# Depthwise images read out of padded maps in SBUF instead of a DRAM copy

## The reference

```python
x = mamba_fuse(x)                      # layer 0: two Mamba blocks, 1x1 fusion, batch norm, + residual x
g = group_norm(x, 32 groups)           # layer 1
d = [dwconv3(g), dwconv5(g), dwconv7(g)]   # depthwise, one 2-D filter per channel, padding SAME
x = x + conv1x1(concat(d))
t = tokens(x)                          # layers 2 and 3: linear attention, then an MLP in fp8 numbers
```

## Time and profile before

| | before |
|---|---|
| median of three runs | 4153.86 us (4151.6 to 4156.21) |
| the profiled execution | 4153.76 us |
| its span | 4152.0 us |
| PE busy | 3542.9 us |
| DVE busy | 3424.4 us |
| ACT busy | 2398.3 us |
| POOL busy | 2838.0 us |
| preparation | 3058 to 3181 us |
| depthwise loop | 3181 to 3395 us |

### The profile page before, as it was taken

One profiled execution on the slowest core, in us unless ns is written; L12 is line 12 of the kernel. 1 busy time (PEld: TensorE's weight loads), 2 busy tenths in 40 slices (PEclk: granted clock), 3 DMA queues, 4 the chain that ended last, 5 costly groups with the idle time before them and its releaser, 6 DMA issues. The chain is left out here.

```text
span 4152.0 us, 38656 instructions
## 1 busy us (share of the span) xinstructions
PE 3542.9 (85%) x10080; PEld 1452.8 (35%) x10080; DVE 3424.4 (82%) x4323; ACT 2398.3 (58%) x4121; POOL 2838.0 (68%) x2328
## 2 busy tenths in 40 slices
PE   6899999999999999999999999998843878686776
PEld 2333333333333333333333333333311336364563
DVE  3999999999999999999999999999971006767676
ACT  5666766766667766666667766666522222425335
POOL 4988889999998889999988899999840000302113
PEclk8999999999999999999999999999976988676565
DMA  2555555555565555555555555555568785100001
GB/s 85 168 160 167 163 156 164 168 157 159 169 170 162 163 157 165 156 157 153 170 160 160 156 155 165 153 154 158 158 165 212 235 231 127 31 16 16 16 1 31
DMA packets 296514, 588.63 MB, mean 142 GB/s; under 512 B 82743, under 2 KB 151994, under 8 KB 295142
## 3 DMA queue, kind: packets, MB, share of 16 engines
q1 hardware_dynamic: 229222, 516.93, 43.0%
q10 hardware_dynamic: 67072, 69.23, 6.5%
HBM read 532.16 MB, written 58.28 MB: 142 GB/s over the span
## 5 line engine op out<-in xcount | busy, mean ns | idle before, releaser
L796 POOL TENSOR_TENSOR prod<-states,c_rows 128x512 f32<-128x512 f32 x1536 | 1927.8, 1282 | 179.1 <-DVE states L726 145.8
L726 DVE TENSOR_TENSOR_SCAN states<-decay,carry,bpsum 128x512 f32<-128x512 f32 x1344 | 1676.9, 1259 | 0.0
L455 PE MATMUL ypsum<-prod,identity 128*128 128x512 f32 x3072 | 1595.1, 602 | 0.5 <-POOL prod L796 0.3
L561 ACT ACTIVATE decay<-delta,decay_rate 128x512 f32<-128x512 f32 x1344 | 934.8, 711 | 313.0 <-DVE states L726 308.6
L706 DVE TENSOR_TENSOR bpsum<-bpsum,dx 128x512 f32<-128x512 f32 x1344 | 904.4, 673 | 138.7 <-PE bpsum L448 124.4
L455 PEld LDWEIGHTS ypsum<-prod,identity 128*128 128x128 f32 x3072 | 583.8, 194 | 422.8 <-issue 281.7
L448 PE MATMUL bpsum<-b_rows,select 96*128 96x512 bf16 x1344 | 522.3, 389 | 210.5 <-DVE states L726 208.0
L1655 POOL TENSOR_TENSOR y<-y,b 128x384 f16<-128x384 f16 x64 | 65.8, 1027 | 912.2 <-ACT y L1465 912.2
L448 PEld LDWEIGHTS bpsum<-b_rows,select 96*128 96x128 bf16 x1344 | 129.4, 96 | 973.3 <-DVE states L726 689.9
L561 ACT ACTIVATE bpsum<-delta,decay_rate 128x512 f32<-128x512 f32 x192 | 132.6, 691 | 309.6 <-DVE states L726 308.7
L495 PE MATMUL mm<-h_norm,w_xs 96*128 96x512 f32 x512 | 262.7, 599 | 6.0 <-ACT h_norm L627 6.0
(11 more groups left out here) (190 smaller groups left out, 4569.1 us busy)
## 6 DMA issues: line engine op xcount, KB each, us to landing
c_rows<-bc_map SPq DMA_DIRECT2D x512, 512.0 KB, 3.8
c_rows<-bc_map SPq DMA_DIRECT2D x512, 256.0 KB, 4.1
b_wide<-bc_map ACTq DMA_DIRECT2D x128, 256.0 KB, 4.6
image<-normed_map SPq DMA_DIRECT2D x192, 96.1 KB
depthwise_map<-dw_sums ACTq DMA_DIRECT2D x96, 192.0 KB, 4.3
dw_parts<-depthwise_map SPq DMA_DIRECT2D x16, 1152.0 KB, 13.2
b_wide<-bc_map ACTq DMA_DIRECT2D x128, 128.0 KB, 4.3
normed_map<-padded SPq DMA_DIRECT2D x8, 1155.0 KB, 12.4
```

Of the source, the lines that this page charges most:

```text
L455: pe.matmul(ypsum[:, group % Y_BANKS, :], identity[:, :], prod[:, n % P_RING, :], start=s == 0, stop=s == STATES - 1).then_inc(summed, 1)
L561: act.activation(into, delta[k % 2][:, g, :], ACT.Exp, scale=decay_rate[:, ORDER[k][0], g, s:s + 1]).then_inc(done, 1)
L726: dve.tensor_tensor_scan(states[:, n % H_RING, :], by, add, carry[:, at, u:u + 1], ALU.mult, ALU.add).then_inc(scanned, 1)
L796: pool.tensor_tensor(prod[:, n % P_RING, :], states[:, n % H_RING, :], c_rows[:, n // C_STATES % C_RING, n % C_STATES, :], ALU.mult).then_ ...
```

## The change

- `img_dram` and the eight stores into it go. `padded` becomes one buffer for all four batches, laid out phase, row, batch, block, column, so that a channel's 44 rows of 560 floats lie one behind the other in the channel's one partition. `load_image` reads them there. Its destination, its two loads a channel and their sizes stay.
- `x0` keeps two buffers instead of four. SP stores batch b to `x0_dram` as soon as its residual is added, on its in-order queue; the load of `x0` for batches 2 and 3 waits until batch 0 or 1 is normalised and stored. The four stores in the depthwise loop go.
- `patch_w` is 96 columns wide instead of 128, so a load's data are contiguous on both sides, and the matmul writes 96 rows instead of 128.
- ACT no longer waits for a free half of `padded`; `norm_ready` counts batches, not halves.
- The image loads begin when all four batches are normalised.

```diff
-            x0 = tmp("x0", [C, BATCH, TOKENS])
+            x0 = tmp("x0", [C, 2, TOKENS])
-            padded = tmp("padded", [C, 2, 2, PATCH_ROWS, ROW_BLOCKS, HALF_ROW])
+            padded = tmp("padded", [C, 2, PATCH_ROWS, BATCH, ROW_BLOCKS, HALF_ROW])
-            patch_w = tmp("patch_w", [128, W_RING, W_CHANNELS, 2, 128])
+            patch_w = tmp("patch_w", [128, W_RING, W_CHANNELS, 2, PATCH_OUT])
...
-                        sp.dma_start(patch_w[0:PATCH, j % W_RING, :, :, 0:PATCH_OUT].rearrange("p c t m -> p (c t) m"),
+                        sp.dma_start(patch_w[0:PATCH, j % W_RING, :, :, :].rearrange("p c t m -> p (c t m)"),
...
+                    lines = padded[:, :, :, :, :, :].rearrange("c f r b n i -> c (f r) (b n i)")
...
-                            sp.dma_start(flat[:, 0:LINE - 1], img_dram[c, :, e:LINE - 1 + e]).then_inc(image_loaded[c % I_RING], 16)
+                            sp.dma_start(flat[:, 0:LINE - 1], lines[c:c + 1, :, e:LINE - 1 + e]).then_inc(image_loaded[c % I_RING], 16)
...
-                    load_f(0)
-                    load_x(0)
-                    load_f(1)
-                    load_x(1)
-                    load_x(2)
+                    def store_x0(b):
+                        sp.wait_ge(x0_added, b + 1)
+                        sp.dma_start(x0_dram[:, b, :], x0[:, b % 2, :]).then_inc(x0_stored[b % 2], 16)
+
+                    for b in range(2):
+                        load_f(b)
+                        load_x(b)
                     for b in range(2, BATCH):
-                        sp.wait_ge(x0_added, b - 1)
+                        store_x0(b - 2)
                         load_f(b)
-                        if b + 1 < BATCH:
-                            load_x(b + 1)
+                        sp.wait_ge(norm_ready, b - 1)
+                        sp.wait_ge(x0_stored[b % 2], 16)
+                        load_x(b)
                     for tile, src in rest:
                         sp.dma_start(tile, src).then_inc(rest_loaded, 16)
                     sp.wait_ge(zeroed, 1)
                     for j in range(W_RING):
                         load_patches(j)
-                    for b in range(BATCH):
-                        for phase in range(2):
-                            sp.wait_ge(norm_ready, 2 * b + phase + 1)
-                            sp.dma_start(img_of[:, phase, :, b, :],
-                                         padded[:, b % 2, phase, :, :, :].rearrange("c r n i -> c r (n i)")).then_inc(img_stored[b % 2], 16)
-                    for i in range(2):
-                        sp.wait_ge(img_stored[i], 32 * BATCH // 2)
+                    for b in range(2, BATCH):
+                        store_x0(b)
+                    sp.wait_ge(norm_ready, BATCH)
...
-                        for b in due(X0_STORE_AT, c):
-                            sp.dma_start(x0_dram[:, b, :], x0[:, b, :]).then_inc(x0_stored, 16)
...
-                            last = pe.matmul(banks[:, c % 4, :].rearrange("m (n i) -> m n i", i=HALF_SIDE),
+                            last = pe.matmul(banks[0:PATCH_OUT, c % 4, :].rearrange("m (n i) -> m n i", i=HALF_SIDE),
...
-                        if b >= 2:
-                            act.wait_ge(img_stored[b % 2], 32 * (b // 2))
...
-                    for i in range(2):
-                        pool.memset(padded[:, i, :, :, :, :].rearrange("c f r n i -> c (f r n i)"), 0.0)
+                    for phase in range(2):
+                        pool.memset(padded[:, phase, :, :, :, :].rearrange("c r b n i -> c (r b n i)"), 0.0)
```

More of the change, by code:

```diff
@@ L857 @@
 W_CHANNELS, LINE = 4, BATCH * ROW_BLOCKS * HALF_ROW
-X0_STORE_AT = (12, 32, 52, 72)
 W_RING, I_RING, O_RING, G_RING = 3, 4, 4, 4
@@ L876, in batch_phase @@
 def batch_phase(nc, dram, f_dram, x0_dram, x_stats, f_stats, out):
-    img_dram = nc.dram_tensor("normed_map", (C, 2 * PATCH_ROWS, LINE), FP32, kind="Internal").ap()
-    img_of = img_dram.rearrange("c (f r) (b n) -> c f r b n", f=2, b=BATCH)
     dw_dram = nc.dram_tensor("depthwise_map", (C, BATCH, PATCH_OUT, ROW_BLOCKS * HALF_SIDE), FP32, kind="Internal").ap()
@@ L930, in batch_phase @@
                      "dev_cast", "const_ready", "first_loaded", "rest_loaded", "fx0_loaded", "fx1_loaded", "fx2_loaded", "fx3_loaded",
-                     "x0_added", "x0_stored", "img0_stored", "img1_stored",
+                     "x0_added", "x0_even_stored", "x0_odd_stored",
                      "mean_ready", "square_ready", "pre_mm", "gn_var", "gn_root", "gn_ready", "norm_ready", "zeroed",
@@ L938, in batch_phase @@
              dev_cast, const_ready, first_loaded, rest_loaded, fx0_loaded, fx1_loaded, fx2_loaded, fx3_loaded,
-             x0_added, x0_stored, img0_stored, img1_stored,
+             x0_added, x0_even_stored, x0_odd_stored,
              mean_ready, square_ready, pre_mm, gn_var, gn_root, gn_ready, norm_ready, zeroed,
@@ L943, in batch_phase @@
              conv_done, evicted, sums0_stored, sums1_stored, sums2_stored, sums3_stored) = handles
-            img_stored = (img0_stored, img1_stored)
+            x0_stored = (x0_even_stored, x0_odd_stored)
             fx_loaded = (fx0_loaded, fx1_loaded, fx2_loaded, fx3_loaded)
@@ L972, in load_patches @@
                             sp.wait_ge(conv_done, W_CHANNELS * (j - W_RING + 1))
-                        sp.dma_start(patch_w[0:PATCH, j % W_RING, :, :, 0:PATCH_OUT].rearrange("p c t m -> p (c t) m"),
+                        sp.dma_start(patch_w[0:PATCH, j % W_RING, :, :, :].rearrange("p c t m -> p (c t m)"),
                                      dram["patch_rows"][:, W_CHANNELS * j:W_CHANNELS * (j + 1), :, :]
-                                     .rearrange("p c t m -> p (c t) m")).then_inc(patch_loaded[j % W_RING], 16)
+                                     .rearrange("p c t m -> p (c t m)")).then_inc(patch_loaded[j % W_RING], 16)
+                    lines = padded[:, :, :, :, :, :].rearrange("c f r b n i -> c (f r) (b n i)")
                     def load_image(c):
@@ L990, in load_x @@
                     def load_x(b):
-                        sp.dma_start(x0[:, b, :], dram["x"][:, b, 0:TOKENS]).then_inc(fx_loaded[b], 16)
-                    load_f(0)
-                    load_x(0)
-                    load_f(1)
-                    load_x(1)
-                    load_x(2)
+                        sp.dma_start(x0[:, b % 2, :], dram["x"][:, b, 0:TOKENS]).then_inc(fx_loaded[b], 16)
+                    def store_x0(b):
[4 more added lines that the diff above has]
+                        load_x(b)
                     for b in range(2, BATCH):
-                        sp.wait_ge(x0_added, b - 1)
+                        store_x0(b - 2)
                         load_f(b)
-                        if b + 1 < BATCH:
-                            load_x(b + 1)
+                        sp.wait_ge(norm_ready, b - 1)
+                        sp.wait_ge(x0_stored[b % 2], 16)
+                        load_x(b)
                     for tile, src in rest:
@@ L1021, in _ @@
                             load_image(c + I_RING)
-                        for b in due(X0_STORE_AT, c):
-                            sp.dma_start(x0_dram[:, b, :], x0[:, b, :]).then_inc(x0_stored, 16)
-                    sp.wait_ge(x0_stored, 16 * BATCH)
+                    for i in range(2):
+                        sp.wait_ge(x0_stored[i], 32)
                 @block.tensor
@@ L1062, in normalise @@
                         act.wait_ge(zeroed, 1)
-                        if b >= 2:
-                            act.wait_ge(img_stored[b % 2], 32 * (b // 2))
-                        rows = x0[:, b, :].rearrange("c (n r w) -> c r n w", n=ROW_BLOCKS, w=SIDE)
+                        rows = x0[:, b % 2, :].rearrange("c (n r w) -> c r n w", n=ROW_BLOCKS, w=SIDE)
                         scale, bias = small[:, b, 6:7], small[:, b, 7:8]
@@ L1068, in normalise @@
                             cols = slice(1 - phase, SIDE, 2)
-                            into = padded[:, b % 2, phase, :, :, 2 - phase:2 - phase + HALF_SIDE]
+                            into = padded[:, phase, :, b, :, 2 - phase:2 - phase + HALF_SIDE]
                             act.activation(into[:, EDGE:EDGE + BLOCK_ROWS, :, :], rows[:, :, :, cols], ACT.Identity, scale=scale, bias=bias)
@@ L1072, in normalise @@
                                            scale=scale, bias=bias)
-                            act.activation(into[:, EDGE + BLOCK_ROWS:, :ROW_BLOCKS - 1, :], rows[:, 0:EDGE, 1:, cols], ACT.Identity,
-                                           scale=scale, bias=bias).then_inc(norm_ready, 1)
+                            last = act.activation(into[:, EDGE + BLOCK_ROWS:, :ROW_BLOCKS - 1, :], rows[:, 0:EDGE, 1:, cols], ACT.Identity,
+                                                  scale=scale, bias=bias)
+                        last.then_inc(norm_ready, 1)
                     act.wait_ge(first_loaded, 16 * len(first))
@@ L1117, in add_residual @@
```

(4 more changed lines are left out.)

## The result

The changed kernel takes 4644.73 us (median of four runs, 4637.82 to 4646.31) where the kernel before took 4155.03 us beside it (median of four, one run more than in the table above): ratio 1.1179, 95% interval 1.1162 to 1.1196. It is 490 us slower. The forecast was 4646 us.

A forecast was written before the change was run, and what follows sets the result against it. DMA transfers were taken to bound the preparation and PE the depthwise loop, then one-partition image loads. Image stream from 3163, plus 718, plus 2 gave 3883 against 3390.84: +492 us on 4153.8, forecast 4646 us, range 4570 to 4890.

The forecast's parts named there:

- The image loads: Depthwise loop: two loads from one partition at 27.4 GB/s take 7.2 us, 7.5 us a channel with other transfers, 718 us.
- A pace that changes from channel to channel: Depthwise loop: sign named beforehand that would show the forecast wrong, as would a loop under 230 us.
- SP's waits for `conv_done`: Depthwise loop: each said to be long over, so the ring of four images does not help; PE sits 5.5 us a channel.
- Rival 1: Depthwise loop: a partition is read as freely as DRAM, loop 187 us, total 4116 us or 4100; chance 0.12.
- rival 2: Depthwise loop: partition shared at the pace of small rows, 12.7 us a channel, total 5147 us; chance 0.06.
- Rival 4: Image loads: only one DMA engine gets the transfer, same 7.2 us and time; part of the forecast, no chance of its own.
- Rival 3: Depthwise loop: between 2.4 and 6.9 us a channel, two or three engines' worth; at 3.6 us 4274 us; chance 0.02.
- The other edits in the loop: Depthwise loop: nothing under slow loads; otherwise 22 us for the moved `x0` stores and at most 16 us for patches.
- The preparation: Before the loop: additions 2 and 3 at 3116 and 3139, maps complete at 3158.4, image stream from 3163, 18 us sooner.
- 7.0 us a map: Preparation: time for each map in SP's queue, read from additions about 14 us apart for two maps; 225 GB/s.
- The zeroing: Preparation: POOL's zeroing of `padded` doubles from 10.4 to 20.9 us, ends near 3087 before it is needed; costs nothing.
- The last stage: After the loop: untouched by the edits; restarting it at a lower clock may cost about 2 us, left to the range.

The follow-up runs named there:

- e9: Changed kernel with one image load a channel instead of two: 4296 us, 3.80 us a channel.
- e2: Changed kernel with its maps stored to DRAM and the images loaded from there: 4143.5 us, ratio 0.9984 to the kernel before.
- e12: Changed kernel with six kinds of image-load source, 16 channels each: 4488 us; 2.27 us a channel from 44 partitions, 4.94 to 7.49 from the others.
- e4: Changed kernel with each channel's second load from the partition 48 further on, same queue: 4381 us, 4.73 us a channel.
- e1: Kernel before with the narrow-patch edits alone: 4147.7 us, ratio 0.9995.
- e5: Changed kernel with each channel's second load on ACT's queue, from the same partition: 4571 us, 6.51 us a channel.
- e6: Changed kernel with each channel's second load on ACT's queue, from the neighbouring partition: 4566 us, 6.47 us a channel.

## Why the prediction was right

**The image loads.** 7.2 us from the sixteenth of 439 GB/s, plus 0.3 for the other transfers, was 7.5; the pace is 7.45. e9 shows that it scales with bytes, e2 that the DRAM source loses nothing, e12 that it belongs to the path of a few partitions. The term was mine by choice between ends far apart: nothing in the trace before told 7.2 from 12.7 us, and the reason given for it, one engine draining one partition, is not what was seen. Seven and a half engines were busy on SP's queue, and the path belongs to a four of partitions and the four 32 on. That such a path gives 27 to 29 GB/s when nothing else is in flight, so near to the sixteenth part of 439, is partly luck.

Two sentences of the prediction did not hold. A pace that changes from channel to channel was to mean that the forecast was wrong, and it did change, from 1.7 to 11.7 us. The loads of four channels are in flight together and land unevenly, while the mean is the forecast one, as e9 and e2 bear out; the sign was badly chosen, but by it alone the forecast would have been given up. And SP's waits for `conv_done` were not long over: 95.0 us of them stood in the loop. They may be why the loop drew 26.4 GB/s on average and not the 27 to 29 of its first images.

**Rival 1**, a partition read as freely as DRAM, and **rival 2**, 12.7 us, did not occur. **Rival 4**, one DMA engine, is excluded by 46.9% of 16 engines on SP's queue, and by e4 and e12, where another source partition alone changed the pace. **Rival 3** did not occur in the changed kernel, but its in-between paces are what two paths give (4.7 to 5.4 us).

**The other edits in the loop.** Worth nothing under the slow loads, as forecast. Without them e2 shows 28.2 us, against 22 for the stores and up to 16 for the patches; e1 puts the patches at nothing that can be told.

**The preparation.** Additions 2 and 3 started at 3113.58 and 3131.18, where 3116 and 3139 were forecast, and the images were issued at 3150.51, not 3158.4 (rows of the changed kernel, DVE, SP and POOL):

```profile
3113.58 4.48 DVE L1114 SCALAR_TENSOR_TENSOR x<-fmap,scale,x 96x4096 f32<-96x4096 f32 x1 [3.01 <-DMA x<-in_x]
...
3131.18 4.48 DVE L1114 SCALAR_TENSOR_TENSOR x<-fmap,scale,x 96x4096 f32<-96x4096 f32 x1 [4.75 <-DMA x<-in_x]
...
3150.51 54.94 SPq L981 DMA_DIRECT2D image<-padded  x14
```

The step that was off is the 7.0 us a map. It was read where only loads ran; with stores beside them the window 3140 to 3150 moved 348 GB/s, half as much again as 225, and the window 3110 to 3120, ahead of addition 3, moved 316:

```profile
3110.00:3120.00 10.00, 0.00 (x0) 0.00 (x0) 6.85 (x8) 6.50 (x7) 0.00 (x0) 0.50 1.03 316
```

So the queue was empty by about 3160 (34 GB/s from there), not 3163, and the first image was under way earlier. The first matmul still came at 3168.53 (forecast 3170): the first channel took 18 us from its issue, with the loads of four channels of the same path in flight beside it. That the first matmul came within 1.5 us of its forecast is thus two errors that cancelled. 3168.53 plus 711 us of loop is 3879.6, where 3883 was forecast.

**The zeroing** was put at nothing and was not quite that; see the last section. **The last stage** took 2.7 us longer (4643.5 - 3879.6 = 763.9 against 4152.0 - 3390.84 = 761.2). The range had given 2 us to a lower clock at its start, and that did not occur. Its first 24 us, before and in the changed kernel:

```profile
3391.00:3415.00 24.00, 10.72 (x18) 3.98 (x19) 1.52 (x3) 0.47 (x1) 0.00 (x0) 0.64 0.89 211
```

```profile
3880.00:3904.00 24.00, 11.53 (x23) 4.37 (x24) 1.52 (x3) 0.23 (x1) 0.00 (x0) 0.72 0.88 213
```

The granted clock was 0.72 against 0.64. The stage took 759.8 to 767.0 us from the last eviction to the end in the fourteen profiled executions, 760.3 behind the slow loop of e4, so 2.7 us can't be told from no change.

## What to carry to other kernels

Before a DRAM tensor is replaced by reads out of SBUF, count how many partitions one transfer reads: transfers out of one partition ran at 26 to 30 GB/s here, with some seven DMA engines busy on them at once, and a neighbour in the same four or the partition 32 on did not add to it. DRAM (1.87 us a channel), or an SBUF source whose rows lie in many partitions (2.27 from 44), gave the same bytes in about a third of the time or less. Price such a load from the narrower side, and set it against the work that it must hide under: below PE's 1.95 us a channel it would have been free.

## What the runs showed of the hardware

- Loads that each read one partition kept seven engines and more busy at once at 26.4 GB/s (196,768 bytes in 7.45 us): a high DMA share is no sign of a high rate.
- Two queues reading the same partition got 30.2 GB/s over the loop, one queue 26.4; but with only one four of partitions in flight both got 27 to 29 (windows of the changed kernel, e5 and e6). The difference was not taken apart further.
- A DVE instruction on 96 x 4 elements took 8.91 us. Rows of the changed kernel, and of the kernel before for the same instruction:

```profile
3062.25 20.69 POOL L1177 MEMSET padded<- 96x12320 f32 x2 [11.51 <-POOLq L850]
...
3074.05 8.91 DVE L1164 TENSOR_SCALAR gpt<-gpt 96x4 f32<-96x4 f32 x1
...
3084.98 4.48 DVE L1114 SCALAR_TENSOR_TENSOR x<-fmap,scale,x 96x4096 f32<-96x4096 f32 x1
```

```profile
3073.54 1.21 DVE L1168 TENSOR_SCALAR gpt<-gpt 96x4 f32<-96x4 f32 x1
```

It ends at 3082.96, POOL's zeroing, two memsets, at 3082.94: DVE stood until the second memset let go, and the first addition began at 3084.98 instead of 3080.94. The 1.21 us before was such a wait too, a short one: it ends at 3074.75, POOL's zeroing of `patch_w` at 3074.72. The Trainium skill (SBUF — State Buffer, Who interferes with whom) says that a `tensor_scalar` can take the port pair that DVE shares with GpSimd and then waits for the whole instruction that holds it; the trace agrees. The longer zeroing thus cost 4 us at that place; what it costs at the end no run took apart.
